# A transformer layer on eight cores: eight PSUM slots and two input buffers in layernorm 1, earlier V transposes, attention transposes three tiles behind, and layernorm 2 emitted one tile ahead

## The reference

```python
x = x + layernorm(attn(layernorm(x), w_qkv, w_out))
x = x + layernorm(ffn(layernorm(x), weight, lora_A, lora_B, router_w))
```

## Time and profile before

| | |
|---|---|
| time, median of 3 runs | 2742.36 us (2741.54 to 2744.57) |
| time of the profiled execution | 2744.7 us |
| its span on the slowest core | 2743.2 us (cores: 2733.2 to 2743.2) |
| TensorE busy | 1822.3 us, 66% |
| ACT busy | 809.1 us, 29% |
| DVE busy | 702.0 us, 26% |
| mean granted TensorE clock | 0.83 |

### The profile page before, as it was taken

One profiled execution on the slowest core, in us unless ns is written; L12 is line 12 of the kernel. 1 busy time (PEld: TensorE's weight loads), 2 busy tenths in 40 slices (PEclk: granted clock), 3 DMA queues, 4 the chain that ended last, 5 costly groups with the idle time before them and its releaser, 6 DMA issues.

```text
span 2743.2 us, 29153 instructions; the slowest of 8 cores (2733.2 to 2743.2 us)
## 1 busy us (share of the span) xinstructions
PE 1822.3 (66%) x9552; PEld 867.7 (32%) x9552; DVE 702.0 (26%) x2241; ACT 809.1 (29%) x1841; POOL 42.1 (2%) x59
## 2 busy tenths in 40 slices
PE   1225788877888888888898882899425353535363
PEld 0112334433444334433443431344112121212121
DVE  4442221112111211212111210344312323232323
ACT  1111432344234432343235431111202222222222
POOL 0000000000000000000000000000000000000000
PEclk9999888988898889888998896999766666667676
DMA  5120111011101111011101006222550000000000
GB/s 115 70 77 31 24 24 21 4 24 24 24 1 24 24 24 14 11 24 24 24 1 24 1 1 108 76 77 76 99 87 16 31 16 31 16 31 16 31 16 31
DMA packets 48657, 95.29 MB, mean 35 GB/s; under 512 B 5248, under 2 KB 38144, under 8 KB 42368
## 3 DMA queue, kind: packets, MB, share of 16 engines
q0 software_dynamic: 46064, 76.58, 14.7%
q1 hardware_dynamic: 2448, 16.85, 1.8%
HBM read 119.67 MB, written 16.78 MB: 50 GB/s over the span
## 4 chain that ended last, share of the span: by engine, by line
PE 57%; DVE 13%; ACT 12%; issue 12%; another core or an unknown queue 4%; DMA 1%; DVEq 1%; ACTq 0%; POOL 0%; SPq 0%; POOLq 0%
PE P_qkv L292 24%; PE P_b L626 9%; ACT expT L379 5%; PE P_qkv L407 5%; DVE sst L150 4%; PE P_e L488 4%; PE P_o L488 4%; PE P_sc L371 2%; PE P_qkv L371 2%; ACT Vaug L332 1%; ACT x2T L591 1%; DVE ost L714 1%; PE P_u L584 1%; PE P_t L326 1%
## 5 line engine op out<-in xcount | busy, mean ns | idle before, releaser
L292 PE MATMUL P_qkv<-A,wbf 128*128 128x512 bf16 x3072 | 668.3, 380 | 13.1 <-DVE att L424 12.6
L292 PEld LDWEIGHTS P_qkv<-A,wbf 128*128 128x128 bf16 x3072 | 300.0, 98 | 376.0 <-issue 18.7
L584 PE MATMUL P_u<-cbuf,xln 128*128 128x128 bf16 x256 | 55.8, 268 | 363.1 <-ACT xln L574 323.6
L626 PE MATMUL P_b<-A,x2T 128*128 128x512 bf16 x1024 | 241.2, 399 | 0.0
L407 PE MATMUL P_qkv<-Vaug,expT 128*128 128x129 bf16 x2176 | 202.0, 253 | 26.4 <-DVE expT L389 25.3
L379 ACT ACTIVATE expT<-P_sc,cbuf 128x512 bf16<-128x512 f32 x320 | 206.3, 712 | 17.3 <-PE P_sc L371 14.2
L379 ACT ACTIVATE expT<-P_qkv,cbuf 128x512 bf16<-128x512 f32 x320 | 208.0, 726 | 0.0
L332 ACT ACTIVATE Vaug<-P_t 128x128 bf16<-128x128 bf16 x256 | 60.9, 279 | 484.4 <-PE P_t L326 481.4
L188 ACT ACTIVATE sst<-sst,cbuf 128x1 f32<-128x1 f32 x64 | 18.8, 294 | 618.1 <-DVE sst L184 618.1
L407 PEld LDWEIGHTS P_qkv<-Vaug,expT 128*128 128x128 bf16 x2176 | 166.8, 114 | 66.0 <-issue 64.6
L249 PE MATMUL P_t<-cbuf,xln 128*128 128x128 bf16 x256 | 51.5, 266 | 192.7 <-ACT xln L240 153.7
(11 more groups left out here) (70 smaller groups left out, 1358.5 us busy)
## 6 DMA issues: line engine op xcount, KB each, us to landing
wbf<-wqkv POOLq DMA_DIRECT2D x16, 1536.0 KB, 15.5
expT<-x SPq DMA_DIRECT2D x16, 1024.0 KB, 5.9
xio<-x POOLq DMA_DIRECT2D x16, 1024.0 KB, 5.2
out<-ost POOLq DMA_DIRECT2D x16, 1024.0 KB, 4.2
wo_bf<-w_out POOLq DMA_DIRECT2D x2, 4096.0 KB, 41.8
A<-weightT POOLq DMA_DIRECT2D x2, 4096.0 KB, 41.1
sat<-at POOLq DMA_DIRECT2D x1, 512.0 KB, 56.7
sbf<-bflat POOLq DMA_DIRECT2D x1, 512.0 KB, 59.7
```

Source lines behind the costliest of these rows:

```text
L292: _q=col0, _p=wpar: e.matmul(P_qkv[:, _q:_q + 512], wbf[:, 6144 * _p + 384 * _c + 128 * _m: 6144 * _p + 384 * _c + 128 * _m + 128], A1[:, ...
L584: e.transpose(_pt[:, 0:128], xln2[:, 2048 * _p + 128 * _c: 2048 * _p + 128 * _c + 128], sid),
L626: e.matmul(P_b[:, 512 * _f:512 * _f + 512], x2T[:, 2048 * _p + 128 * _c: 2048 * _p + 128 * _c + 128], A2[:, 2048 * _c + 512 * _f: 2048 * _ ...
```

## The change

It does five things.

- Layernorm 1 has two input buffers, so the load of tile t+1 no longer waits for `xln` of tile t.
- Its transposes go round eight PSUM slots, one in each bank, instead of two.
- Each V transpose waits only for the cast of its own block of 512 tokens.
- `att` has four buffers and the reciprocal four columns of its own, `srcp`; the transposes of `att` are held back by three AV products instead of one.
- Layernorm 2 of tile t+1 is emitted between the router matmuls and the base matmuls of tile t, instead of at the start of its own tile. In the queues of DVE and ACT it so stands ahead of the router chain of tile t.

```diff
-            xio = expT[:, 0:4096].bitcast(F32)
+            xio2slot = expT[:, 0:8192].bitcast(F32)
...
+            ln1_slots = [P_qkv[:, 0:512].bitcast(BF16),
+                         P_qkv[:, 512:1024].bitcast(BF16),
+                         P_qkv[:, 1024:1536].bitcast(BF16),
+                         P_qkv[:, 1536:2048].bitcast(BF16),
+                         P_sc[:, 0:512].bitcast(BF16),
+                         P_sc[:, 512:1024].bitcast(BF16),
+                         P_t1, P_t2]
...
+                xio = xio2slot[:, 2048 * par:2048 * par + 2048]
+                xsem = c["ld_x0"] if par == 0 else c["ld_x1"]
...
-                    waits=B.gw(["xio"]), inc=c["ld_x"], inck=16)
+                    waits=B.gw([("xio", par)]), inc=xsem, inck=16)
...
-                    pt = P_t1 if ch % 2 == 0 else P_t2
-                    bank = 6 + ch % 2
+                    slot = ln1_slots[(16 * t + ch) % 8]
+                    bank = (16 * t + ch) % 8
...
+                                if m == 2:
+                                    vt_block[2 * half + tb] = dv
...
-                        waits=[(c["dve"], vt_dve)] + B.gw([bank]), inc=c["pe"])
+                        waits=[(c["dve"], vt_block[k // 4])] + B.gw([bank]),
+                        inc=c["pe"])
...
-                        apar = qt % 2
+                        apar = qt % 4
...
-                                        stc(_p, 36),
+                                        srcp[:, _p:_p + 1],
...
-                        if len(pend_T) > 1:
+                        if len(pend_T) > 3:
                             drain_T(pend_T.pop(0))
...
-            for t in range(NT):
+            def plan_ln2(t):
                 par = t % 2
                 rstd, negmr, dve_ln = plan_ln(
...
+            xl2_next = plan_ln2(0)
+            for t in range(NT):
+                par = t % 2
+                xl2 = xl2_next
...
                 aux_done = c["pe"].v
+                if t + 1 < NT:
+                    xl2_next = plan_ln2(t + 1)
                 gw_base = B.gw([0, 1, 2, 3])
```

More of the change, by code:

```diff
@@ L43, in __init__ @@
         self.c = {n: Ctr(nc, n) for n in
-                  ("ld_c", "ld_x", "ld_w0", "ld_w1", "ld_wo", "ld_wt",
+                  ("ld_c", "ld_x0", "ld_x1", "ld_w0", "ld_w1", "ld_wo", "ld_wt",
                    "ldg", "out0", "out1", "pe", "act", "dve", "pool")}
@@ L128, in build_program @@
         sst = en(nc.sbuf_tensor("sst", [128, 2 * 40], F32))
+        srcp = en(nc.sbuf_tensor("srcp", [128, 4], F32))
         B = Builder(nc)
@@ L150, in plan_ln @@
                         e.bn_stats(sst[:, _b + 6 * _j: _b + 6 * _j + 6], _f(_j))),
-                       waits=(list(pre_waits) + B.gw([("sst", par), ("rcp", par)])) if j == 0 else (),
+                       waits=(list(pre_waits) + B.gw([("sst", par)])) if j == 0 else (),
                        inc=(c["dve"] if j == 3 else None))
@@ L196, in plan_ln @@
                         waits=[(c["act"], av)], inc=c["dve"])
-            B.sg([("sst", par), ("rcp", par)], c["dve"], dv)
+            B.sg([("sst", par)], c["dve"], dv)
             return stc(par, 37), stc(par, 38), dv
@@ L218, in build_program @@
             VTs = pen(nc.sbuf_tensor("VTs", [128, 2048], BF16))
-            att = pen(nc.sbuf_tensor("att", [128, 2 * 128], BF16))
+            att = pen(nc.sbuf_tensor("att", [128, 4 * 128], BF16))
             Vaug = pen(nc.sbuf_tensor("Vaug", [128, 16 * 129], BF16))
             expT = pen(nc.sbuf_tensor("expT", [128, 16 * 512], BF16))
-            xio = expT[:, 0:4096].bitcast(F32)
+            xio2slot = expT[:, 0:8192].bitcast(F32)
             P_qkv = pen(nc.psum_tensor("P_qkv", [128, 2048], F32))
@@ L229, in build_program @@
                                inc=c["dve"])
+            ln1_slots = [P_qkv[:, 0:512].bitcast(BF16),
[5 more added lines that the diff above has]
+                         P_t1, P_t2]
             for t in range(NT):
                 par = t % 2
-                xrdy = B.emit("sync", lambda s, _t=t: s.dma_start(
-                    out=xio, in_=x_in[128 * _t:128 * _t + 128, :]),
-                    waits=B.gw(["xio"]), inc=c["ld_x"], inck=16)
@@ L236, in build_program @@
-                rstd, negmr, dve_ln = plan_ln(
[L237 to L241, removed]
+                xio = xio2slot[:, 2048 * par:2048 * par + 2048]
+                xsem = c["ld_x0"] if par == 0 else c["ld_x1"]
@@ new lines, in build_program @@
+                xrdy = B.emit("sync", lambda s, _t=t, _x=xio: s.dma_start(
+                    out=_x, in_=x_in[128 * _t:128 * _t + 128, :]),
+                    waits=B.gw([("xio", par)]), inc=xsem, inck=16)
+                rstd, negmr, dve_ln = plan_ln(
+                    (lambda j, _x=xio: _x[:, 512 * j: 512 * j + 512]), par,
+                    pre_waits=[(xsem, xrdy)])
+                xlv = B.emit("scalar", lambda e, _p=par, _r=rstd, _m=negmr,
+                             _x=xio: e.activation(
+                                 xln[:, 2048 * _p:2048 * _p + 2048],
+                                 _x, AF.Identity, bias=_m, scale=_r),
@@ L242, in build_program @@
                              waits=[(c["dve"], dve_ln)] + B.gw([("xln", par)]),
                              inc=c["act"])
-                B.sg(["xio"], c["act"], xlv)
+                B.sg([("xio", par)], c["act"], xlv)
                 for ch in range(NCH):
-                    pt = P_t1 if ch % 2 == 0 else P_t2
-                    bank = 6 + ch % 2
-                    tv = B.emit("tensor", lambda e, _p=par, _c=ch, _pt=pt:
+                    slot = ln1_slots[(16 * t + ch) % 8]
+                    bank = (16 * t + ch) % 8
+                    tv = B.emit("tensor", lambda e, _p=par, _c=ch, _pt=slot:
@@ L254, in build_program @@
                                 + B.gw([bank]), inc=c["pe"])
-                    dv = B.emit("vector", lambda e, _t=t, _c=ch, _pt=pt:
+                    dv = B.emit("vector", lambda e, _t=t, _c=ch, _pt=slot:
                                 e.tensor_copy(
@@ L319, in build_program @@
                                 B.sg([2 * half + tb], c["dve"], dv)
+                                if m == 2:
+                                    vt_block[2 * half + tb] = dv
+                    if m == 1:
+                        vt_block = [0, 0, 0, 0]
                 B.sg([("wbf", wpar)], c["pe"], c["pe"].v)
@@ L426, in build_program @@
                                           P_qkv[:, _a:_a + 128],
-                                          stc(_p, 36), None, ALU.mult),
+                                          srcp[:, _p:_p + 1], None, ALU.mult),
                                       waits=[(c["dve"], fv)]
@@ L572, in build_program @@
                     par, pre_waits=B.gw([("x2", t)]))
[L573 to L579, removed]
+                return B.emit("scalar", lambda e, _p=par, _t=t, _r=rstd,
+                              _m=negmr: e.activation(
+                                  xln2[:, 2048 * _p:2048 * _p + 2048],
+                                  A1[:, 2048 * _t:2048 * _t + 2048],
+                                  AF.Identity, bias=_m, scale=_r),
+                              waits=[(c["dve"], dve_ln)]
+                              + B.gw([("xln2", par)]), inc=c["act"])
+            xl2_next = plan_ln2(0)
+            for t in range(NT):
+                par = t % 2
+                xl2 = xl2_next
                 for ch in range(NCH):
```

## The result

The kernel after takes 2469.4 us (median of 10 runs) where the kernel before takes 2744.3: the ratio is 0.900, with a 95% interval of 0.898 to 0.902, so 275 us are saved. The prediction said 2490 us, 251 saved, with a range from 2470 to 2524.

A forecast was written before the change was run, and what follows sets the result against it. Each stage was taken as a chain through several engines, none full; savings of 164 (layernorm 2), 53 (layernorm 1), 15 (V wait) and 19 us (attention transposes) sum to 251, from 2742.4 to 2490 us, range 2470 to 2524.

The forecast's parts named there:

- Attention transposes three behind: Attention: the transpose ending a phase no longer waits for the att just computed; 19 us saved, bounds 5.7 to 28.
- the V wait: Attention: V transposes no longer wait for the last cast of V, once a head; 15.1 us saved, bounds 0 to 15.
- Layernorm 1: First stage: eight PSUM slots save 48 us and two input buffers 5 us, together 53 us.
- rival A: Layernorm 1 and attention: DVE copies don't overlap, each taking 0.22 us or more; 219 us saved, 2523 us; chance 0.10.
- Rival B: Layernorm 1: the input load becomes the bound, tile period stays 14.4 us; 53 us lost, 2543 us; chance 0.03.
- Layernorm 2 ahead: Feed-forward: 10.93 us between x2s and the first x2T copy saved in each of 15 tile transitions, 164 us.
- The cover: Feed-forward: router chain, delayed by the moved layernorm 2, still ends 9 us before the su transpose needs it.
- rival C: Feed-forward: moved layernorm 2 doesn't hide and the base matmuls' tail waits; up to 120 us back, 2610 us; chance 0.04.
- D: Whole kernel slower: shorter pieces of work leave the matrix streams at the 1.2 GHz clock; 2750 us; chance 0.01.
- combined bounds: Whole kernel: the bounds of all terms taken together, 2469 to 2540 us.

The follow-up runs named there:

- the fastest version: Kernel after, with V and feed-forward transposes in groups of four, next tile's transposes among the last base matmuls, layernorm 2 two tiles ahead: 2225.9 us, ratio 0.8102.

## Why the prediction fell short

**The failed step is the sizing of the attention terms.** In the prediction, "Attention transposes three behind" is worth 19 us, "0.4 us in three of four phases, and 0 for the fourth", and the V wait 15.1 us. Alone they measured 28.5 and 20 us, and in the change the stage gave 48 instead of 34, 14 of the missing 24 us. Which waits go and where the others move was right; the two prices were too low, for two reasons.

First, idle time in a wait row begins at the recorded end of a matmul, which lies behind the moment when the next one could be issued. For the V wait this makes 0.94 us out of 1.10 (shown by the run with that part alone), and 15.1 us, which I also took as the upper bound, lay just below the measured interval of 16 to 24.

Second, I looked only at the transpose at the phase's end. One that stood between the wait for DVE and the next AV product also leaves the chain. In the kernel before, these rows stand around the product of four matmuls in the earlier trace rows:

```profile
655.15 0.27 PE L346 MATMUL P_t<-cbuf,att 128*128 128x128 bf16 x1 [1.32 <-DVE sst L418]
655.28 0.48 PE L407 MATMUL P_qkv<-Vaug,expT 128*128 128x129 bf16 x3
...
656.81 1.06 PE L371 MATMUL P_sc<-Qbf,Kbf 128*128 128x512 bf16 x2
```

And here is the same phase in the kernel after, of the head whose projection starts at 621.66:

```profile
673.54 0.48 PE L423 MATMUL P_qkv<-Vaug,expT 128*128 128x129 bf16 x3 [1.32 <-DVE srcp L434]
673.81 0.31 PE L362 MATMUL P_t<-cbuf,att 128*128 128x128 bf16 x1
673.96 0.60 PE L423 MATMUL P_qkv<-Vaug,expT 128*128 128x129 bf16 x4
674.35 0.31 PE L362 MATMUL P_t<-cbuf,att 128*128 128x128 bf16 x1
674.46 1.06 PE L387 MATMUL P_sc<-Qbf,Kbf 128*128 128x512 bf16 x2
```

The AV product now starts straight from the wait. From the end of the wait to the last product it is 0.42 us (673.96 less 673.54) where it was 0.70 (655.85 less 655.15), and from there to the scores 0.50 us (674.46 less 673.96) where it was 0.96 (656.81 less 655.85). The second saving, 0.46 us, is the one that the prediction priced, at 0.53 for this phase; the first, 0.28 us, it didn't count. In the mean over heads the four AV parts became shorter by 0.68, 0.55, 0.44 and 0.15 us, as the expectation of the run with that part says: 1.8 us a head and not 1.2. That two steps of distance give as much as three shows that the prediction's account of which wait goes and which stays was right.

**Layernorm 1: right sum, wrong shares.** 53 us forecast, 57 measured. The copies overlap, with starts 0.13 us apart, so rival A falls. The prediction quoted the Trainium skill (VectorE: DVE Perf Modes, "The DRAIN you can't avoid"), by which the next operation does not start until the pipe is empty; the same paragraph goes on: "A next op that is not held starts earlier" (held means made to wait until every earlier one has finished). The trace agrees with this second sentence: four copies take 0.62 us where one takes 0.22, for these copies out of PSUM, of which none reads what another wrote. The statistics start 2.48 us behind the first transpose where the sum had 2.85. But the prediction credited 48 us to the slots and 5 to the buffers, and the slots alone gave 17. It set the load's 5.9 us against the new tile period, as for a load asked for a tile ahead, without asking what the load would do with one buffer, where it is a parallel branch from the end of xln. That the sum still came out is owed to both parts being in the change, and not to the shares. Rival B, the load as bound, is what one buffer shows (13.4 us a tile); with two it is gone.

**Layernorm 2 ahead: right.** 164 us forecast, 170 measured, 171 with this part alone. The 6 us more have two halves. I left 0.1 us from the end of x2s to the first x2T copy, and the copy's record starts 0.09 us before that end (2182.19 against 2180.28 + 2.00), 0.19 us a tile or 3 us. And the base matmuls of the fifteen tiles fell from 14.9 to 14.7 us in the mean of the chain's rows, another 3. The cover was right to 0.4 us, and a different order in the queues changed nothing; rival C falls. So does D: the granted clock of the attention went from 0.88 to 0.89.

**The range.** Its low end was cut to 2470, beside combined bounds of 2469, and two of the four upper bounds (15 for V, 56 for layernorm 1) weren't bounds: 20 and 57 to 60 came; a third, 28 for the attention transposes, was just reached. All errors lie on one side, but not for one reason: idle time read from a wait row accounts for the V wait alone, 2.5 us (17.6 less 15.1). That the others add to them instead of cancelling is in part chance.

**What stays open.** No share of the clock that comes only with both parts together shows in the attention, since the savings a head add up within the scatter of the cores (3.01 against 3.08 us, or 3.28 against 3.05). With the V part alone heads came 1.37 us closer together, 1.10 of which lies at the wait. The granted clock from the first to the last projection was 0.90 in that run and 0.88 before; whether that is the other 0.27 us, or only scatter between cores, no run shows.

## What to carry to other kernels

Price a wait of TensorE from start to start, over the whole loop, with the mean of all turns: the idle time in a wait row starts at a recorded end that lies behind the next possible start, and one turn need not be the mean. When two resources are freed in one change, ask what each does while the other is still scarce; here PSUM slots gave 17 us, the second buffer 4, and both 60. And when an instruction leaves the place between a wait and the work behind it, its own duration leaves the chain too.

## What was not expected of the hardware

The loads of x landed in 4.8 us (median; 4.6 at the least) on the slowest core of the run with eight slots and one buffer, where the slowest core of the kernel before has 5.9 and 5.7. The cores differ: in the kernel before the medians of four of them are 4.7 or 4.8 us and those of the other four 5.5 to 5.9, while with eight slots and one buffer all eight lie between 4.7 and 4.9; why, no run here shows. It matters for the slots alone: an estimate from these rows is that a load of 5.9 us would have made each tile 1.1 us longer and left next to nothing of the 17 us.

One ACT copy of 512 columns out of one PSUM bank took 0.60 us, and it is the same whether the target is contiguous (`x2T`) or lies in blocks 129 apart (`Vaug`). From the fastest version, minimum, median and maximum in ns, and three copies in a row:

```profile
L352 ACT ACTIVATE Vaug<-P_t x64: 593/598/601, 229.8 to 1464.4; 128x512 bf16<-128x512 bf16 x64
...
L618 ACT ACTIVATE x2T<-P_u x64: 591/597/659, 1802.9 to 2185.1; 128x512 bf16<-128x512 bf16 x64
```

```profile
1917.08 1.87 ACT L618 ACTIVATE x2T<-P_u 128x512 bf16<-128x512 bf16 x3
```

16 single copies, with their transposes, took 6.3 us a head in the kernel after, and grouping them by four, here and in the feed-forward tiles, made the kernel 108 us faster in all.
